# Moving the second column half of a batched FFN from the middle steps of an eight-item pipeline to its start and end

## Chip, cores and metric

The kernel runs on one core of one Trainium2 chip. The metric is the device time of one execution in microseconds (us), as the median of three runs.

## The reference

Eight items of 256 tokens and 256 features pass through one "macaron" block each:

```
x = x + 0.5 * ffn(layernorm(x))                   # first FFN
x = x + attn(layernorm(x))                        # mamba mixer, then a gated MLP (1024 wide)
x = x + 0.5 * ffn(layernorm(x))                   # second FFN, same weights as the first
ffn(x) = sum over 32 experts of combine[t,e] * (silu(x wg_e) * (x wu_e)) wd_e   # top 6 of 32, 96 wide
         + (silu(x sg) * (x su)) sd                                             # shared, 192 wide
```

combine is made from the sigmoid of x @ gate_w: the six largest of the 32 scores, divided by their sum. The mamba mixer has an input projection, a causal convolution of four taps, a recurrence over the tokens with 16 states for each of 512 channels, a gate, and an output projection. All of it is float32.

## The kernel before

**Layout.** Features lie on the partitions, tokens on the free axis, so one item is a tile of 128 x 2 x 256. The FFN is computed densely: 26 chunks of 128 hidden units (24 routed, 2 shared). For each chunk TensorE makes a gate half and an up half, 6 matmuls each (L737 to L739: the weight and the input are each split in a high and a low part, three products, two k blocks), ScalarE takes the tanh (L980) and copies the up half (L970), VectorE applies the gate (L1107, item by_g), GpSimd multiplies by the up half (L1376, by_u) and by the routing weight (L1384, by_comb), and TensorE adds the down projection into the two banks acc (L818; each of the two shows as 2 records, 4 per chunk). All of these work on columns `spans[s.n]` of tiles that are 512 columns wide: 256 columns are one item's call, 512 columns are two calls side by side that share the weights. Below, "narrow" is 256 columns and "wide" is 512.

**Steps.** items_of(t) gives the order of work of step t, for t from -1 to 9. Item i's stages are spread over steps: its first FFN (call f1) in step i, its mamba part in step i+1, its MLP and later its second FFN (call f2 or f2a) in steps i+2 and i+3. So in a middle step four items are in work. Two lists, the heavy one (MLP, then FFN) and the light one (mamba, norms, routing), are merged by fixed weights (merge, WEIGHT, SPACE), and every engine follows the merged order strictly, with a fixed lag for VectorE and GpSimd.

The column slots are filled like this:

| step | columns | first slot | second slot | other work |
|---|---|---|---|---|
| 0 | 256 | f1 of item 0 | - | the FFN weights arrive and are split (ws), the halves go to DRAM (keep_w) |
| 1 | 512 | f1 of item 1 | f1 of item 2 | mamba of item 0 with its own front; no MLP |
| 2 | 256 | f1 of item 3 | - | mamba of item 1 with its own front, first half of item 2's front, MLP of item 0 |
| 3 to 6 | 512 | f1 of items 4 to 7 | f2 of items 0 to 3 | mamba, first half of the next item's front, MLP |
| 7 | 512 | f2a of item 5 | f2 of item 4 | the same; f2a needs the MLP of its own step, a norm and a routing first |
| 8 | 256 | f2a of item 6 | - | mamba of item 7, MLP of item 6, norm and routing |
| 9 | 256 | f2a of item 7 | - | MLP of item 7, norm and routing |

The "front" of an item is what comes before its recurrence: norms lnA or lnO and rms1 or rmsO, projections (L885), convolution, softplus. It has two halves, front(0) and front(1). front(0, "own") stands at the head of a step, before its units, because the item's first FFN ended only with the step before. front(0, "next") stands among units 16 to 31 of the step before. The recurrence is 32 units (ub and unit: L912, L1262, L1069, L1271, L915, L1277, L1397). Items 0 to 7 are read and normed ahead of their first FFN (norm ln1 and ln1b, routing of 8 short pieces on VectorE).

**x1.** The result of the first FFN is added to x. For steps 0 and 1 it lies in x1. The later ones are made in x1_next and moved to x1 by an SBUF to SBUF transfer in the next step (item "shift", L707), which waits until the residual base res has been read (r0, L1153); then x for the next item is loaded to x1_next (again_n, L711). x2kept holds an item between its MLP and its second FFN.

**Queues.** SyncE issues all transfers but the MLP weights, in the order of the merged list: input, weight halves (L672), fronts' spreads (L680 to L689), shift and again_n, stores. GpSimd issues the MLP weights.

Of the kernel before, what the change touches and what calls it, by code (L numbers as in the profile page):

```python
# [67 lines left out]
    "again_n": {"x_again_n": 16},  # L68
    "shift": {"shifted": 16},
# [51 lines left out]
STARTS = {"x2_free": 16}  # L121
# [30 lines left out]
def routing(call):  # L152
    return [("rt1", call)] + [("rq", call, i) for i in range(len(ROUTE))]
# [59 lines left out]

def items_of(t):


    if t < 0:
        return [("load", 0)] + norm("ln1") + routing("f1")
# [3 lines left out]

    first, twin, second, own = t < BATCH - 1, t == 1, 3 <= t < BATCH, t >= BATCH - 1
    late_front, next_front = 1 <= t <= 2, 2 <= t < BATCH
    ready = (["f1"] if first else []) + (["f2"] if twin or second else [])
    hand = [("hx", call) for call in ready] + [("rt2", call) for call in ready]
    following = t == 0 or t + 2 < BATCH
    keep = [("keep",)] if second else []  # L230
    keep += [("load", 0)] if following else []
# [4 lines left out]
    ln1 = norm("ln1") + routing("f1") if following else []  # L236
    if t == 0:
        ln1 = ln1[:2] + [("load", 1)] + ln1[2:] + norm("ln1b") + routing("f2")
    ahead = [(k, c) for c in range(MSLOTS) for k in ("mgn", "mdn")] if 0 <= t + 1 - 2 < BATCH else []
    ff = ffn_items(t)  # L240
    if not mamba:
        if t == 0:
            return hand + keep + merge(ff[:-TAIL], turn + ln1, WEIGHT) + ahead + ff[-TAIL:]
        return mlp_items() + ahead + norm("ln2a") + routing("f1") + [("rt2", "f1"), ("hx", "f1")] + ff
    follow = norm("lnA") + norm("rms1") + merge(front(0, "next"), ln2, SPACE) if next_front else ln2
    light = norm("lnO") + norm("rmsO") + front(0, "own") if late_front else []
    begin = len(light)
# [3 lines left out]
    turns = [("end", "mlp")] if mlp else []  # L251
    turns += [("nm", "lnO")] if late_front else []
    if not mlp:
        out = hand + keep + merge(ff[:-TAIL], light, WEIGHT) + ahead + ff[-TAIL:]
    elif own:
        chain = mlp_items() + ahead + norm("ln2a") + routing("f1") + [("rt2", "f1"), ("hx", "f1")]
        cut = begin + len(unit_items(0) + front(1, "own")) * 2 // 3
        out = hand + keep + merge(chain, light[:cut], WEIGHT) + merge(ff[:-TAIL], light[cut:], WEIGHT) + ff[-TAIL:]
    else:
        heavy = mlp_items() + ahead + ff  # L260
        out = hand + heavy[:6] + keep + merge(heavy[6:-TAIL], light, WEIGHT) + heavy[-TAIL:]
    out = near(after(out, turn, *turns))
    if next_front:

        at = out.index
        assert at(("shift",)) < at(("n1", "lnA")) and at(("ub", UNITS // 2)) < at(("split", 0, "next"))
        assert at(("yz", 1)) < min(at(("xc", 0, "next", 0)), at(("z", 0, "next")))
# [55 lines left out]
def ffn_items(t):  # L323
# [6 lines left out]
    for p in range(FFN_CHUNKS + DLAG):  # L330
        now, before = p < FFN_CHUNKS, 1 <= p <= FFN_CHUNKS
        out += [("cmb", "ff", p // 3)] if p < ROUTED and p % 3 == 0 else []
        out += [("g", "ff", p)] if now else []
        out += [("by_u", "ff", p - 1)] if before else []
        out += [("by_comb", "ff", p - 1)] if 1 <= p <= ROUTED else []
# [10 lines left out]
    if t < BATCH - 1:  # L346
        out += [("end", "f1" if t < 2 else "f1n")]
    if t == 1:
        out += [("end", "f1b")]
    if 3 <= t < BATCH:  # L350
        out += [("end", "f2"), ("store",)]
    return out + ([("end", "f2a"), ("store_own",)] if t >= BATCH - 1 else [])


# [80 lines left out]
def macaron_kernel(nc, d):  # L435
# [8 lines left out]
    spans = [(0, 2 * SEQ if t == 1 or 3 <= t < BATCH else SEQ) for t in times]  # L444
# [3 lines left out]
    with ctx:  # L448
# [29 lines left out]
        x1_next = sb("x1_next", [P, KC, SEQ])  # L478
# [38 lines left out]
        parts = sb("parts", [P, PARTS, 2, SEQ], BF16)  # L517
        rows = nc.dram_tensor("rows", [3, P, PARTS, 2, SEQ], BF16, kind="Internal").ap()
# [105 lines left out]
        def _(sp):  # L624
# [6 lines left out]
            def do(s, it):  # L631
                if it[0] == "load":
# [87 lines left out]
            sp.wait_ge(sem["x2_free"], STARTS["x2_free"] + 16 * BATCH)  # L720
# [3 lines left out]
        def _(pe):  # L724
# [18 lines left out]
            def do(s, it):  # L743
# [77 lines left out]
                elif kind_of(it) == "n1c":  # L821
# [4 lines left out]
                    elif it[1] == "lnA":  # L826
                        pe.wait_ge(sem["shifted"], s.count("shifted", ("shift",), 16))
# [18 lines left out]
                elif kind == "rt1":  # L846
                    if s.n == 0:
                        pe.wait_ge(w_small, 16 * 4)
                    norm = next(n for n in NORMS_OF[it[1]] if ("nm", n) in s.at)
                    pe.wait_ge(sem["normed"], s.count("normed", ("nm", norm), 1))  # L850
# [9 lines left out]
                elif kind == "rt2":  # L860
# [6 lines left out]
                    for tt in range(TT):  # L867
# [615 lines left out]
```

## Time and profile before

| | |
|---|---|
| median of 3 runs | 1793.62 us (1792.89 to 1794.39) |
| the profiled execution | 1797.3 us, span 1795.5 us from first to last instruction |
| PE busy | 1556.8 us, 87% |
| DVE busy | 1288.6 us, 72% |
| POOL busy | 993.8 us, 55% |
| ACT busy | 842.9 us, 47% |
| mean granted TensorE clock | 0.947 |
| bytes moved | 200.25 MB, mean 112 GB/s |

PE is TensorE's matmuls, PEld its weight loads (they overlap PE), DVE VectorE, ACT ScalarE, POOL GpSimd, SPq SyncE's queue of transfers. Busy PE time is modelled and includes stretches at half clock. A step is taken here from the end of the FFN's residual of the step before (L1133) to its own. The next heading's rows are word for word from the profile; L737 is line 737 of the kernel above.

### The profile page before, as it was taken

To read this page: it belongs to the slowest core of one execution; us is meant where nothing else is said; L and a number is where in the kernel's file an instruction comes from. 1 tells how busy PE (TensorE), PEld (TensorE's weight loads), DVE (VectorE), ACT (ScalarE), POOL (GpSimd) and SP (SyncE) were. 2 spreads that over 40 slices of the span, in tenths; PEclk is the share of its full clock that TensorE was granted. 3 is DMA by queue.
4 is the path that set the end of the run, shared out by engine and by line. 5 is a ranking of instruction groups with operands and counts; after the bars stand their busy time and mean duration, and the time that the engine had idled before them with its cause. 6 is when DMAs were issued, how large, how long until landed. Compare 5 with 4: busy or idle time off the path is not lost. (4 is left out here: it accounts for less than half of the span.)

```text
span 1795.5 us, 22504 instructions
## 1 busy us (share of the span) xinstructions
PE 1556.8 (87%) x7088; PEld 1136.3 (63%) x7088; DVE 1288.6 (72%) x2085; ACT 842.9 (47%) x1676; POOL 993.8 (55%) x1048
## 2 busy tenths in 40 slices
PE   6878888777788999899998999899985999868979
PEld 5756555655676666666666666666663666647868
DVE  4536995478968878687959887887857776679421
ACT  4434543545624563356534663456433553445323
POOL 2523676345545766376646666476633766348525
PEclk9989999978989999999999999999996999979989
DMA  6863223332332323242333223232321332224434
GB/s 220 318 206 98 78 82 101 96 100 85 101 105 90 115 84 110 70 138 78 111 102 118 83 90 112 85 129 84 105 79 41 123 100 102 82 86 158 145 104 147
DMA packets 72278, 200.25 MB, mean 112 GB/s; under 512 B 9921, under 2 KB 22433, under 8 KB 71777
## 3 DMA queue, kind: packets, MB, share of 16 engines
q1 hardware_dynamic: 63968, 173.65, 29.1%
q0 software_dynamic: 8192, 25.17, 4.8%
q8 instruction: 57, 0.93, 0.2%
q14 instruction: 61, 0.49, 0.1%
HBM read 173.62 MB, written 23.59 MB: 110 GB/s over the span
## 5 line engine op out<-in xcount | busy, mean ns | idle before, releaser
L737 PE MATMUL gub<-x_hi,wr 128*128 128x512 f32 (+1 forms) x1040 | 425.4, 409 | 50.6 <-DVE hid L1107 44.8
L1397 POOL TENSOR_TENSOR ring<-ring 128x512 f32<-128x512 f32 x192 | 253.6, 1321 | 307.4 <-DVE ring L1277 306.2
L1376 POOL TENSOR_TENSOR hid<-hid,u_sb 128x512 f32<-128x512 f32 (+1 forms) x260 | 289.6, 1114 | 236.1 <-ACT u_sb L970 199.0
L818 PE MATMUL acc<-hid,w_down 128*128 128x512 f32 (+1 forms) x1040 | 408.9, 519 | 1.8 <-POOL hid L1376 1.8
L739 PE MATMUL gub<-x_hi,wr 128*128 128x512 f32 (+1 forms) x1040 | 370.8, 357 | 0.0
L738 PE MATMUL gub<-x_lo,wr 128*128 128x512 f32 (+1 forms) x1040 | 370.2, 356 | 0.0
L1271 DVE TENSOR_TENSOR_SCAN ring<-decays,side 128x512 f32<-128x512 f32 x256 | 310.5, 1213 | 28.9 <-ACT decays L1069 24.6
L970 ACT ACTIVATE u_sb<-gub 128x512 f32<-128x512 f32 (+1 forms) x260 | 132.7, 510 | 347.3 <-PE gub L739 346.8
L980 ACT ACTIVATE hid<-gub 128x256 f32<-128x256 f32 (+1 forms) x324 | 156.8, 484 | 278.2 <-PE gub L739 153.7
L1384 POOL TENSOR_TENSOR hid<-hid,weight 128x512 f32<-128x512 f32 (+1 forms) x240 | 272.9, 1137 | 15.8
L737 PEld LDWEIGHTS gub<-x_hi,wr 128*128 128x128 f32 x1040 | 205.4, 197 | 93.6 <-issue 58.1
L818 PEld LDWEIGHTS acc<-hid,w_down 128*128 128x128 f32 x1040 | 189.2, 197 | 97.2 <-issue 80.8
L1069 ACT ACTIVATE decays<-dts,a_neg 128x255 f32<-128x255 f32 x512 | 228.8, 497 | 3.8 <-DVE ring L1271 3.6
L1262 DVE TENSOR_TENSOR side<-dtx,side 128x512 f32<-128x512 f32 x256 | 176.8, 690 | 69.0 <-PE side L912 68.3
L739 PEld LDWEIGHTS gub<-x_hi,wr 128*128 128x128 f32 x1040 | 204.6, 197 | 27.1
L738 PEld LDWEIGHTS gub<-x_lo,wr 128*128 128x128 f32 x1040 | 205.8, 198 | 24.4 <-issue 5.5
L1107 DVE SCALAR_TENSOR_TENSOR hid<-hid,gub 128x512 f32<-128x512 f32 (+1 forms) x260 | 149.0, 573 | 98.3 <-ACT hid L980 98.3
L1277 DVE TENSOR_TENSOR ring<-ring,side 128x512 f32<-128x512 f32 x256 | 176.0, 687 | 59.5 <-PE side L915 36.2
L885 PE MATMUL side<-rn,w_in 128*128 128x256 f32 x448 | 120.4, 417 | 18.7 <-DVE ring L1271 13.5
L912 PE MATMUL side<-bst,sel_b 96*128 96x256 bf16 x512 | 103.7, 285 | 33.9 <-DVE ring L1271 18.1
L915 PE MATMUL side<-cst,sel_c 96*128 96x256 bf16 x512 | 103.9, 286 | 33.2 <-DVE ring L1271 32.7
L779 PE MATMUL gub<-xn_mlp,wm_gu 128*128 128x256 f32 x512 | 122.4, 387 | 0.0
(120 smaller groups left out, 1823.3 us busy)
## 6 DMA issues: line engine op xcount, KB each, us to landing
wr<-w_halves SPq DMA_DIRECT2D x234, 512.0 KB, 3.3
wm_gu<-in_w_mlp POOLq DMA_DIRECT2D x64, 256.0 KB, 3.1
w_halves<-wr SPq DMA_DIRECT2D x26, 512.0 KB, 4.9
wm_down<-in_w_mlp POOLq DMA_DIRECT2D x64, 128.0 KB, 2.6
w_raw<-in_w_gu SPq DMA_DIRECT2D x26, 256.0 KB, 4.3
rows<-parts SPq DMA_DIRECT2D x16, 384.0 KB, 2.3
cst<-rows SPq DMA_DIRECT2D x48, 128.0 KB, 2.6
xin<-in_x SPq DMA_DIRECT2D x8, 256.0 KB, 2.9
```

Source lines behind the costliest of these rows:

```text
L737: mm(out, w[:, 0, half, k, :], x_hi[:, k, a:b], start=(k == 0), stop=False)
L738: mm(out, w[:, 0, half, k, :], x_lo[:, k, a:b], start=False, stop=False)
L739: last = mm(out, w[:, 1, half, k, :], x_hi[:, k, a:b], start=False, stop=(k == KC - 1))
L818: last = mm(acc[k][:, a:b], w, h[:, a:b], start=(c == 0), stop=(c == (MLP_CHUNKS if mlp else FFN_CHUNKS) - 1))
L980: A(hid[c % HSLOTS][:, a:b], s.gub_of(it)[:, a:b], ACT.Tanh, scale=0.5).then_inc(sem["tanh_done"], 1)
L1069: A(decay[u % 2][:, h, 1:SEQ], dts[:, j, 1:SEQ], ACT.Exp, scale=a_neg[:, j, n:n + 1]).then_inc(sem["decay"], 1)
L1262: v.tensor_tensor(b, twice(dtx[:, j, :]), b, ALU.mult).then_inc(sem["driven"], 1)
L1271: v.tensor_tensor_scan(w.rearrange("p h s -> p (h s)"), decay[u % 2][:, :, :].rearrange("p h s -> p (h s)"), s.side_of(("ub", u))[:, :], 0 ...
L1277: v.tensor_tensor(w, w, pair(s.side_of(it)), ALU.mult).then_inc(sem["read_out"], 1)
L1376: nc.gpsimd.tensor_tensor(h, h, u_sb[c % USLOTS][:, a:b], ALU.mult).then_inc(sem["hidden"], 1)
L1384: nc.gpsimd.tensor_tensor(h, h, weight[c // 3 % CSLOTS][:, a:b], ALU.mult).then_inc(sem["weighted"], 1)
L1397: add(ysum, ysum, ring[:, u % 3], ALU.add).then_inc(sem["y_sum"], 1)
```

## The change

The columns are dealt out anew. Items 0 to 5 have their first FFN in pairs, in steps 0, 1 and 2, at 512 columns. Steps 3 to 8 run at 384 columns: one slot of a whole item and one of half an item's tokens (128). Step 9 stays at 256.

| step | columns before | columns after | calls after |
|---|---|---|---|
| 0 | 256 | 512 | f1 of items 0, 1 |
| 1 | 512 | 512 | f1 of items 2, 3 |
| 2 | 256 | 512 | f1 of items 4, 5 |
| 3, 4 | 512 | 384 | half of f1 of item 6, f2 of items 0, 1 |
| 5, 6 | 512 | 384 | half of f1 of item 7, f2 of items 2, 3 |
| 7 | 512 | 384 | half of f2 of item 5 (its own MLP first), f2 of item 4 |
| 8 | 256 | 384 | half of f2 of item 5, f2 of item 6 (its own MLP first) |
| 9 | 256 | 256 | f2 of item 7 |

With items 0 and 1 both ready after step 0, front(0, "next") starts in step 1, and only step 1 still has front(0, "own"). The norms and routings that must be ready move too: items 0 and 1 before step 0 (their routing inside step 0), 2 and 3 in step 0, 4 and 5 in step 1, 6 in step 2, 7 in step 4. x1 of all items but item 0 goes to a DRAM tensor x1_kept (store_a, store_b at a step's end) and comes back by a transfer "fetch" at the place of shift. x for the residual is loaded at the head of steps (again_a, again_b). The memset of x2kept at the start is gone.

```
+FIRST = {0: (0, 1), 1: (2, 3), 2: (4, 5), 3: (6,), 4: (6,), 5: (7,), 6: (7,)}
+NORMED_IN = {-1: (0, 1), 0: (2, 3), 1: (4, 5), 2: (6,), 4: (7,)}
+OWN_SLOT = {BATCH - 1: "f1", BATCH: "f2", BATCH + 1: "f1"}
+def half_of(t):
+    return (t - 3) % 2 if 3 <= t <= BATCH else None
+def span_of(t):
+    return (0, 2 * SEQ) if t < 3 else (P, 2 * SEQ) if t <= BATCH else (0, SEQ)
+def place(t, slot):
+    if slot == "f2":
+        return slice(SEQ, 2 * SEQ), slice(0, SEQ)
+    half = half_of(t)
+    return (slice(0, SEQ), slice(0, SEQ)) if half is None else (slice(P, SEQ), slice(half * P, half * P + P))
...
-    late_front, next_front = 1 <= t <= 2, 2 <= t < BATCH
+    next_front = 1 <= t < BATCH
...
-    turn += [("again",)] if t < 2 else [("shift",)] if t < BATCH else []
-    turn += [("again_n",)] if 1 <= t < BATCH - 1 else []
+    turn += [("fetch",)] if next_front else []
...
+    if t == 0:
+        early = [it for call in ("f1", "f2") for it in routing(call, ("early",)) + [("rt2", call)]]
+        at = ff.index(("cmb", "ff", 0))
+        return near(fetches + hand + merge(ff[:at], early, WEIGHT) +
+                    merge(ff[at:-TAIL], ln1, WEIGHT) + ahead + ff[-TAIL:])
...
+        late = splits and p < 3
+        if late and p == 2:
+            out += [("cmb", "ff", 0), ("by_comb", "ff", 0), ("by_comb", "ff", 1)]
...
-    spans = [(0, 2 * SEQ if t == 1 or 3 <= t < BATCH else SEQ) for t in times]
+    spans = [span_of(t) for t in times]
...
-                if it[0] == "shift":
+                if it[0] == "fetch":
                     sp.wait_ge(sem["r_base"], s.count("r_base", ("r0",), 1))
-                    sp.dma_start(x1[:], x1_next[:]).then_inc(sem["shifted"], 16)
+                    stored = "b_stored" if s.t() in (1, 3, 5) else "a_stored"
+                    sp.wait_ge(sem[stored], s.prior(stored))
+                    sp.dma_start(x1[:], x1_kept[s.t()]).then_inc(sem["fetched"], 16)
+                if it[0] == "again_a":
+                    if (least := s.prior("a_stored")) is not None:
+                        sp.wait_ge(sem["a_stored"], least)
+                    sp.dma_start(x1_stage[:], d["x"][FIRST[s.t()][0]]).then_inc(sem["x_again_a"], 16)
+                if it[0] == "store_a":
+                    sp.wait_ge(sem["residual"], s.count("residual", ("end", "f1n"), KC))
+                    sp.dma_start(x1_kept[FIRST[s.t()][0]], x1_stage[:]).then_inc(sem["a_stored"], 16)
...
-            v.memset(x2kept[:], 0.0).then_inc(sem["x2_free"], STARTS["x2_free"])
...
-                        v.scalar_tensor_tensor(dst[:, k, :], acc[k][:, a:a + SEQ], scale, src[:, k, :],
+                        v.scalar_tensor_tensor(dst[:, k, tokens], acc[k][:, cols], scale, src[:, k, tokens],
```

## Rows read from the trace of the kernel before

**Rows 1.** Windows by step: length, busy PE PEld DVE ACT POOL, PEclk, DMA share, GB/s.

```profile
0.00:116.00 116.00, 84.89 (x478) 75.68 (x478) 50.00 (x136) 47.82 (x106) 42.96 (x54) 0.93 0.75 259
116.00:314.90 198.90, 171.62 (x674) 111.72 (x675) 144.65 (x210) 93.81 (x177) 113.00 (x98) 0.95 0.30 98
314.90:528.60 213.70, 160.56 (x826) 132.29 (x825) 162.91 (x270) 104.72 (x218) 95.49 (x118) 0.87 0.31 98
528.60:727.60 199.00, 185.16 (x784) 126.80 (x784) 159.66 (x251) 101.28 (x191) 121.90 (x118) 0.99 0.30 97
...
1125.70:1324.60 198.90, 182.29 (x764) 123.87 (x763) 155.62 (x228) 97.79 (x185) 122.10 (x118) 0.99 0.31 99
1324.60:1537.70 213.10, 187.43 (x764) 127.76 (x764) 152.07 (x227) 97.66 (x185) 121.37 (x118) 0.94 0.28 91
1537.70:1694.00 156.30, 123.90 (x714) 103.13 (x712) 120.73 (x196) 67.35 (x158) 90.37 (x118) 0.89 0.36 117
...
sum 1793.20, PE 1556.78 PEld 1136.32 DVE 1288.56 ACT 842.89 POOL 993.75; mean PE 155.68 PEld 113.63 DVE 128.86 ACT 84.29 POOL 99.38
```

**Rows 2.** Windows of stretches inside steps; same columns.

```profile
361.50:436.80 75.30, 55.42 (x294) 44.34 (x293) 66.20 (x104) 34.73 (x79) 37.66 (x39) 0.82 0.31 100
436.80:507.60 70.80, 53.79 (x297) 44.65 (x298) 63.70 (x101) 41.67 (x88) 36.31 (x38) 0.88 0.29 94
507.60:528.60 21.00, 16.16 (x82) 13.75 (x81) 10.98 (x20) 5.68 (x10) 6.62 (x8) 0.92 0.31 104
528.60:567.20 38.60, 29.70 (x139) 23.65 (x139) 29.90 (x53) 15.00 (x32) 12.76 (x25) 0.96 0.18 52
567.20:618.70 51.50, 51.05 (x224) 34.37 (x221) 49.12 (x78) 28.40 (x55) 42.99 (x43) 1.00 0.43 141
618.70:700.90 82.20, 78.61 (x330) 51.68 (x330) 67.55 (x102) 49.75 (x93) 54.96 (x43) 1.00 0.30 97
700.90:727.60 26.70, 25.80 (x96) 17.09 (x95) 13.09 (x22) 8.13 (x12) 11.19 (x10) 1.00 0.24 79
1125.70:1158.40 32.70, 26.88 (x132) 21.26 (x131) 27.12 (x49) 14.43 (x33) 12.50 (x24) 0.97 0.25 72
...
1386.80:1537.70 150.90, 149.14 (x592) 99.68 (x592) 102.67 (x133) 72.53 (x135) 97.57 (x76) 0.98 0.31 103
...
1600.00:1694.00 94.00, 83.52 (x543) 72.90 (x542) 73.33 (x107) 42.57 (x108) 66.66 (x76) 0.96 0.47 155
```

**Rows 3.** Timeline of PE, narrow call: start, length, what.

```profile
1760.10 1.02 PE L818 MATMUL acc<-hid,w_down 128*128 128x256 f32 x4
...
1762.39 1.02 PE L818 MATMUL acc<-hid,w_down 128*128 128x256 f32 x4
```

**Rows 4.** Timeline of PE, wide call.

```profile
640.51 0.39 PE L737 MATMUL gub<-x_hi,wr 128*128 128x512 f32 x1
640.74 0.39 PE L738 MATMUL gub<-x_lo,wr 128*128 128x512 f32 x1
...
643.04 1.88 PE L818 MATMUL acc<-hid,w_down 128*128 128x512 f32 x4
644.76 1.89 PE L885 MATMUL side<-rn,w_in 128*128 128x256 f32 x8
```

**Rows 5.** Groups by line and shape, DVE: busy us, mean ns, idle before.

```profile
L1107 DVE SCALAR_TENSOR_TENSOR hid<-hid,gub 128x512 f32<-128x512 f32 x156 | 105.9, 679 | 32.9 <-ACT hid L980 32.9
...
L1107 DVE SCALAR_TENSOR_TENSOR hid<-hid,gub 128x256 f32<-128x256 f32 x104 | 43.1, 415 | 65.3 <-ACT hid L980 65.3
```

**Rows 6.** Timeline of the start, three instructions.

```profile
4.24 2.04 PE L835 MATMUL side<-xin,mean_w 128*128 128x256 f32 x4 [4.24 <-DMA xin<-in_x]
...
12.21 0.69 DVE L1176 TENSOR_TENSOR xc_f<-xc_f,rstd 128x512 f32<-128x512 f32 x1 [5.13 <-ACT rstd L998]
...
22.32 0.78 PE L737 MATMUL gub<-x_hi,wr 128*128 128x256 f32 x1
```

**Rows 7.** Waits in 22 to 116 us: total us, times, longest.

```profile
ACT wr L949 <- DMA w_raw<-in_w_gu: 19.5, 7, 5.1
```

More of the change, by code:

```diff
@@ L67 @@
     "again": {"x_again": 16},
-    "again_n": {"x_again_n": 16},
-    "shift": {"shifted": 16},
+    "again_a": {"x_again_a": 16},
+    "again_b": {"x_again_b": 16},
+    "store_a": {"a_stored": 16},
+    "store_b": {"b_stored": 16},
+    "fetch": {"fetched": 16},
     "hx": {"x_hi": 1, "x_split": 1},
@@ L119 @@
 }
[L121 removed]
+STARTS = {}
 def kind_of(item):
@@ L214, in items_of @@
 def items_of(t):
     if t < 0:
-        return [("load", 0)] + norm("ln1") + routing("f1")
+        ln1 = norm("ln1")
+        return [("load", 0)] + ln1[:2] + [("load", 1)] + ln1[2:] + norm("ln1b")
     mamba, mlp = 0 <= t - 1 < BATCH, 0 <= t - 2 < BATCH
-    first, twin, second, own = t < BATCH - 1, t == 1, 3 <= t < BATCH, t >= BATCH - 1
-    late_front, next_front = 1 <= t <= 2, 2 <= t < BATCH
-    ready = (["f1"] if first else []) + (["f2"] if twin or second else [])
-    hand = [("hx", call) for call in ready] + [("rt2", call) for call in ready]
@@ L229, in items_of @@
-    following = t == 0 or t + 2 < BATCH
-    keep = [("keep",)] if second else []
-    keep += [("load", 0)] if following else []
+    own = OWN_SLOT.get(t)
+    next_front = 1 <= t < BATCH
+    ready = [slot for slot in ("f1", "f2") if slot != own and t <= BATCH]
+    hand = [("hx", call) for call in ready]
+    hand += [("rt2", call) for call in ready] if t else []
+    keep = [("keep",)] if 3 <= t <= BATCH else []
+    fetches = ([("again",), ("again_b",)] if t == 0 else [("again_a",), ("again_b",)] if t < 3 else
+               [("again_a",)] if t in (3, 5) else [])
@@ L239, in items_of @@
+    ln1 = [("load", 0)] + ln1 if ln1 else []
+    if t in NORMED_IN and len(NORMED_IN[t]) > 1:
+        ln1 = ln1[:3] + [("load", 1)] + ln1[3:] + norm("ln1b") + routing("f2")
     ahead = [(k, c) for c in range(MSLOTS) for k in ("mgn", "mdn")] if 0 <= t + 1 - 2 < BATCH else []
     ff = ffn_items(t)
[L241 to L244, printed above, removed]
+    if t == 0:
[3 more added lines that the diff above has]
+                    merge(ff[at:-TAIL], ln1, WEIGHT) + ahead + ff[-TAIL:])
@@ L245, in items_of @@
+    chain = []
+    if own:
+        chain = (norm("ln2a") + routing("f1") if own == "f1" else norm("ln2") + routing("f2")) + [
+            ("rt2", own), ("hx", own)]
+        chain = mlp_items() + ahead + chain
+        if not mamba:
+            return chain + ff
     follow = norm("lnA") + norm("rms1") + merge(front(0, "next"), ln2, SPACE) if next_front else ln2
-    light = norm("lnO") + norm("rmsO") + front(0, "own") if late_front else []
-    begin = len(light)
+    light = norm("lnO") + norm("rmsO") + front(0, "own") if t == 1 else []
@@ L265, in items_of @@
         at = out.index
-        assert at(("shift",)) < at(("n1", "lnA")) and at(("ub", UNITS // 2)) < at(("split", 0, "next"))
+        assert at(("fetch",)) < at(("n1", "lnA")) and at(("ub", UNITS // 2)) < at(("split", 0, "next"))
         assert at(("yz", 1)) < min(at(("xc", 0, "next", 0)), at(("z", 0, "next")))
@@ L826, in do @@
                     elif it[1] == "lnA":
-                        pe.wait_ge(sem["shifted"], s.count("shifted", ("shift",), 16))
+                        pe.wait_ge(sem["fetched"], s.count("fetched", ("fetch",), 16))
                     elif it[1] == "lnO":
@@ L846, in do @@
                 elif kind == "rt1":
[L847 removed]
+                    if s.n == 1:
                         pe.wait_ge(w_small, 16 * 4)
[L849 to L850 removed]
+                    pe.wait_ge(sem["normed"], s.count("normed", it, 0))
                     for over, least in s.last_use("side", it):
```

90 lines of the change are left out of this document (50 added, 40 removed).

## The prediction

> **What bounds the kernel now.** I read the windows by step first. Over the ten steps PE is busy 1557 of 1793 us and DVE 1289 [rows 1], so the means name TensorE. The steps differ. Step 3 has PE busy 185 of 199 us, and step 6, with fewer DVE instructions (228 against 251), takes the same 198.9 us: those wide middle steps follow PE. Step 2 computes half as many FFN columns and still takes 213.7 us, with PE at 161 and DVE at 163. Steps 0 and 8 are narrow too and have PE idle for 31 and 32 us. So columns are crowded where PE has no slack and missing where it has.
>
> Then the stretches inside a step [rows 2]. Step 3 (start at 528.6) has four: MLP until the first FFN matmul, 38.6 us with DVE at 29.9 and PE at 29.7, a chain of short dependent pieces, bound by neither; 51.5 us up to scan 16, where PE is 99% and DVE 95% busy; 82.2 us up to scan 31 with PE at 96% and DVE at 82%; a tail of 26.7 us with PE at 97%. The same three last stretches of step 2, narrow, take 75.3 (all of units 0 to 15), 70.8 and 21.0 us, and in the first two DVE is at 88 and 90%, PE at 74 and 76%. So at 256 columns the units are bound by VectorE, at 512 by TensorE, and 384 lies near the crossing. That is the question of this change.
>
> **What a column costs.** Narrow chunks follow each other by 2.29 us on a dense PE (start of one chunk's down matmuls to the next's, 12 gate and up matmuls between) [rows 3]. Wide: gate and up matmuls start 0.23 us apart, and four down records take 644.76 - 643.04 = 1.72 us [rows 4], so a chunk is 12 x 0.23 + 1.72 = 4.48 us. 26 chunks: 59.5 us narrow, 116.5 us wide. That is linear in columns with nearly no fixed part, so 384 columns are estimated halfway, 88 us, and no weight load sets a floor. The change keeps ten FFN passes and 4096 columns in all. PE's work is the same to a microsecond: all that can be won or lost is idle time. The term on DVE, by_g, is 679 ns wide and 415 narrow [rows 5], so 547 at 384: 26 x 0.132 = 3.4 us less per step.
>
> **Step 0, 256 to 512 columns.** Before, the FFN waits for weights (19.5 us of ScalarE waiting for w_raw [rows 7], DMA share 0.75 [rows 1]): 90 us for 59.5 us of PE work. Wide, PE needs 116.5, plus some 2 us of routing-weight matmuls and 7.5 us for two norms and four routings, 126 us, longer than the 90 us in which the weights came; they are hidden. The start is later: the first norm's chain runs from 4.24 to 12.9 us [rows 6], the second follows with its ScalarE part behind the first, about 8 us, then two splits (1.1 us each) and the first weight split: first gate matmul near 24 instead of 22.3. Routing of both calls is moved behind the first matmuls. End: 24.5 + 126/0.96 + 3 = 158 against 116. **+42** (37 if PE never waits, 50 if weights still cost 8).
>
> **Step 1, still 512.** It gains front(0, "next") and a second norm with routing. What that costs DVE is read from steps 1 and 2: step 2 has those same two things (its second norm is ln2) and the MLP's 16 gatings, and is narrow by 26 x 0.264 = 6.9 us, which the MLP's 16 x 0.42 = 6.7 offsets. So step 1 gets step 2's DVE load, 162.9 us instead of 144.7, while PE goes from 172 to about 184. With step 2's ratio of span to DVE time (213.7/162.9) it takes 214, with step 1's own (198.9/144.7) 224; I take 217, nearer the lower as the kinds of work are step 2's. **+18** (8 if it is PE at 184/0.89 = 207, 30 if the added chain is bare).
>
> **Step 2, 256 to 512.** The own front leaves its head. What is left is step 3's list but for f1 in the second slot. 199. **-14.7** (-12 to -16).
>
> **Steps 3 to 6, 512 to 384.** PE loses 28.5 us per step, 1.1 per chunk; DVE 3.4. By stretches: MLP 38.6, unchanged. To scan 16, ten chunks: PE 51 - 11 = 40, DVE 49.1 - 1.3 = 48; DVE binds, 50 us (-1.5). To scan 31, twelve chunks: PE 78.6 - 13 = 65.5, DVE 67.6 - 1.6 = 66. Bounds: 82.2 (nothing won) and 66/0.95 = 69.5, 0.95 being DVE's share in the stretch before; step 2's DVE share of 0.90 gives 73. I take 72 (-10). Tail: midway of 26.7 and 21.0, 24 (-3). Sum 184.5. Three of the four steps no longer hold a first norm: step 6, which has none, has an MLP stretch of 32.7 instead of 38.6 [rows 2], lost again later to PE before. Now PE has room, so I count 5 of those 6: 179.5. Four steps: 184.5 + 3 x 179.5 = 723 against 796. **-73** (-92 if stretches meet their DVE floor at once, -39 by the clock, below).
>
> **Step 7, 512 to 384.** From the first FFN matmul on, 150.9 us with PE at 149.1 and DVE only at 102.7 [rows 2]. PE goes to 120.6, DVE to 99. At 95% of PE: 127. **-24** (-28 to -15). **Step 8, 256 to 384.** From 1600 on, 94 us with PE at 83.5; PE goes to 112, over 0.97: 115.5. **+22** (18 to 28.5, the whole of the added work). **Step 9**: 0.
>
> **x1 by DRAM.** Fetch stands where shift stood, behind the same wait for r0, and moves the same 256 KB. What waits for it is lnA, among units 16 to 31, some 60 us later. The stores at a step's end queue ahead of again_a and again_b (each waits for a store to land, a few us) and those ahead of weight loads whose chunks are 6 ahead, at least 13 us. Cover: 38 us of MLP in steps 3 to 7; in steps 1 and 2 the slots already filled. Cost 0; if the cover failed, 2 to 4 us in each of two steps. again_n's load, which stood before a weight load right after shift, is gone from there.
>
> **Sum.** 42 + 18 - 15 - 73 - 24 + 22 = -30. The profiled span of 1795.5 becomes 1766; its own time was 1797.3, the median 1793.6. Taking 30 from the median: **1764 us**.
>
> **Rivals.** (1) Clock. In step 2's narrow unit stretches the granted clock is 0.82 and 0.88, in step 3's wide ones 1.00 [rows 2]: a PE left with gaps falls between its two levels of 2.4 and 1.2 GHz, and the same matmul takes twice as long. If 384 columns leave gaps like step 2's, the stretches become 40/0.82 = 49 to 52 us, 65.5/0.88 = 74.4 to 77, tail 25: 192.6 and 188 without the norm, four steps 757. The sum is -30 + 34 = +4: **1798**, slower. It decides if the four steps lose less than 9 us each on average. Against it: PE would be 80% busy there, more than step 2's 75%, and DVE's 66 us leave room for a slowed PE up to 0.99 of it. The Trainium skill, "TensorE: Matmul & The Clock Gate", section "HAM oscillation", says that a kernel whose matmul bursts are separated by short idle gaps keeps falling back to half rate; by that rule alone the sum would be this rival's. The trace agrees at 256 columns and shows none of it at 512; no row is at 384. (2) DVE and PE, near balance under a fixed order that was weighted for 512 columns, hinder each other: the long stretch stays at 78, steps 3 to 6 give 45 to 50: **1785** or so. For it: step 2 never reaches 0.95 of DVE. Against: step 3 has both at 95 and 99% for 51 us. (3) PE bound all along: units shrink to their DVE floor, the full MLP saving stays, steps 3 to 6 give 92: **1746**. (4) Zero sum: what steps 3 to 7 give, steps 0, 1 and 8 take, as PE's work is the same: **1793**. Against it is the 31 us of idle PE in step 0 and the front that leaves step 2's head.
>
> **Chances.** My sum, within 11 us: 0.47. Rival 3 side (1735 to 1753): 0.14. Rival 2 side (1775 to 1790): 0.23. Rival 4: 0.06. Rival 1: 0.10. Range 1745 to 1789; the likeliest alone 1753 to 1775. A difference of 0.2% (3.6 us) is what a measurement of this kernel can tell. Faster 0.84, same 0.06, slower 0.10.
>
> **What would show it.** Right: step 0 near 158 us with PE dense; step 1 near 217; step 2 at 199; steps 3, 5, 6 at 180 and step 4 at 185, DVE at 90% or more up to scan 31; step 7 at 189, step 8 at 178; fetch landing long before lnA. Wrong: PEclk under 0.92 in steps 3 to 6; the stretch to scan 31 near 80 us; step 1 over 225; SPq's weight loads late after again_a.

## The result: slower by 2.1% where a gain of 1.7% was forecast

| | before | after |
|---|---|---|
| median | 1794.01 us | 1831.60 us (1826.90 to 1834.43) |
| ratio | | 1.0206, 95% interval 1.0183 to 1.0230 |
| profiled span | 1795.5 us | 1829.6 us |
| mean granted clock | 0.947 | 0.944 |

The forecast was 1764 with a range of 1745 to 1789. The change made the kernel 38 us slower. The sign was wrong, and rival 1, the only one with that sign, gave 1798.

The windows by step of the changed kernel, cut as [rows 1] are, at the end of the FFN's residual (length; then busy PE, PEld, DVE, ACT, POOL; PEclk, DMA share, GB/s):

```profile
0.00:159.80 159.80, 139.84 (x496) 93.97 (x496) 77.19 (x164) 67.09 (x112) 71.02 (x54) 0.99 0.59 198
159.80:391.10 231.30, 190.06 (x739) 127.15 (x740) 168.51 (x257) 115.39 (x210) 115.10 (x98) 0.93 0.26 86
391.10:605.70 214.60, 194.34 (x777) 131.96 (x776) 162.62 (x250) 101.32 (x191) 120.93 (x118) 0.94 0.30 98
605.70:790.50 184.80, 159.12 (x768) 123.87 (x767) 148.13 (x228) 90.56 (x185) 107.56 (x118) 0.97 0.33 107
790.50:992.00 201.50, 168.69 (x778) 130.17 (x777) 154.63 (x252) 94.93 (x191) 107.61 (x118) 0.92 0.30 99
992.00:1175.80 183.80, 159.88 (x768) 124.86 (x767) 147.99 (x229) 90.74 (x185) 107.61 (x118) 0.96 0.33 107
1175.80:1364.40 188.60, 159.34 (x761) 123.77 (x760) 150.62 (x228) 90.00 (x185) 107.42 (x118) 0.96 0.32 104
1364.40:1553.50 189.10, 161.70 (x767) 126.84 (x766) 146.94 (x228) 90.98 (x185) 107.49 (x118) 0.92 0.32 103
1553.50:1727.30 173.80, 148.33 (x717) 115.59 (x716) 127.45 (x203) 74.26 (x158) 103.97 (x118) 0.92 0.32 104
...
sum 1827.20, PE 1569.33 PEld 1177.99 DVE 1309.64 ACT 844.90 POOL 992.06; mean PE 156.93 PEld 117.80 DVE 130.96 ACT 84.49 POOL 99.21
```

Set beside the forecast step by step, most of the ledger holds. Step 0 is 159.8 (forecast 158) with PE dense, step 7 is 189.1 (189), step 8 is 173.8 (178), steps 3 and 5 are 184.8 and 183.8 (179.5). The error sits in four steps: step 1 at 231.3 (217), step 2 at 214.6 (199), step 4 at 201.5 (184.5), step 6 at 188.6 (179.5). Step 2 is the telling one. It was to be a copy of step 3 before, the same number of columns and the same work, 199.0 us [rows 1], and it takes 15.6 us more with a clock of 0.94 against 0.99. Steps 3 and 6 do the same work as each other and differ by 3.8 us. In sum the steps are 64 us over the forecast span of 1766: step 0 by 2, step 1 by 14, step 2 by 16, steps 3 to 6 by 36, step 8 under it by 4.

### The profile page after: what moved, and what is told of

The parts are those of the page before. It is cut to its first block and busy times, and to the rows that moved or that the text cites. A ratio compares the mean times of both kernels' runs of the same rounds, so it can differ in the third digit from the quotient of the medians.

```text
span 1829.6 us, 22541 instructions
## 1 busy us (share of the span) xinstructions
PE 1569.3 (86%) x7088; PEld 1178.0 (64%) x7088; DVE 1309.6 (72%) x2100; ACT 844.9 (46%) x1676; POOL 992.1 (54%) x1048
## 5 line engine op out<-in xcount | busy, mean ns | idle before, releaser
L789 PE MATMUL gub<-x_hi,wr 128*128 128x384 f32 (+2 forms) x1040 | 435.0, 418 | 36.5 <-DVE hid L1158 33.8
L1435 POOL TENSOR_TENSOR hid<-hid,u_sb 128x384 f32<-128x384 f32 (+2 forms) x260 | 288.7, 1110 | 253.6 <-ACT u_sb L1022 246.7
L870 PE MATMUL acc<-hid,w_down 128*128 128x384 f32 (+2 forms) x1040 | 404.5, 514 | 0.4 <-POOL hid L1435 0.4
L791 PE MATMUL gub<-x_hi,wr 128*128 128x384 f32 (+2 forms) x1040 | 372.4, 358 | 0.0
L790 PE MATMUL gub<-x_lo,wr 128*128 128x384 f32 (+2 forms) x1040 | 372.1, 358 | 0.0
L1022 ACT ACTIVATE u_sb<-gub 128x384 f32<-128x384 f32 (+2 forms) x260 | 132.3, 509 | 363.2 <-PE gub L791 362.7
L1032 ACT ACTIVATE hid<-gub 128x384 f32<-128x384 f32 (+2 forms) x324 | 156.9, 484 | 301.8 <-PE gub L791 165.6
L1443 POOL TENSOR_TENSOR hid<-hid,weight 128x384 f32<-128x384 f32 (+2 forms) x240 | 271.6, 1132 | 20.8 <-ACT weight L1012 5.6
L789 PEld LDWEIGHTS gub<-x_hi,wr 128*128 128x128 f32 x1040 | 203.3, 196 | 74.4 <-issue 50.1
L1158 DVE SCALAR_TENSOR_TENSOR hid<-hid,gub 128x384 f32<-128x384 f32 (+2 forms) x260 | 149.1, 574 | 90.0 <-ACT hid L1032 89.9
L791 PEld LDWEIGHTS gub<-x_hi,wr 128*128 128x128 f32 x1040 | 202.6, 195 | 14.2
L937 PE MATMUL side<-rn,w_in 128*128 128x256 f32 x448 | 118.4, 412 | 15.0 <-DVE ring L1330 13.4
```

What stands on the lines that cost most here:

```text
L789: mm(out, w[:, 0, half, k, :], x_hi[:, k, a:b], start=(k == 0), stop=False)
L790: mm(out, w[:, 0, half, k, :], x_lo[:, k, a:b], start=False, stop=False)
L791: last = mm(out, w[:, 1, half, k, :], x_hi[:, k, a:b], start=False, stop=(k == KC - 1))
L870: last = mm(acc[k][:, a:b], w, h[:, a:b], start=(c == 0), stop=(c == (MLP_CHUNKS if mlp else FFN_CHUNKS) - 1))
L1032: A(hid[c % HSLOTS][:, a:b], s.gub_of(it)[:, a:b], ACT.Tanh, scale=0.5).then_inc(sem["tanh_done"], 1)
L1435: nc.gpsimd.tensor_tensor(h, h, u_sb[c % USLOTS][:, a:b], ALU.mult).then_inc(sem["hidden"], 1)
```

## What the trace shows first: a load that stands right in front of its reader

The instructions on the tile xin, the item read for the first norm, in the changed kernel (the matmul row; then the DMA whose landing ended idle time before these instructions, the idle us and how often):

```profile
L887 PE MATMUL side<-xin,mean_w x32: 377/558/796, 4.2 to 852.4; 128*128 128x256 f32 x32
...
  DMA xin<-in_x: 28.6, 8
```

and in the kernel before:

```profile
L835 PE MATMUL side<-xin,mean_w x32: 377/379/765, 4.2 to 984.5; 128*128 128x256 f32 x32
...
  DMA xin<-in_x: 4.2, 1
```

Before, the one wait for this transfer is that of the first instructions. After, the idle time counts PE and its weight loads; of PE alone it is 4.2 us at the start and then 3.9, 2.4 and 5.1 us in steps 1, 2 and 4, the only steps behind step 0 that have such norms. Step 4 after, timeline of SyncE and then of PE (start, length, what):

```profile
843.35 1.63 SPq L711 DMA_DIRECT2D wr<-w_halves  x3
845.02 0.43 SPq L678 DMA_DIRECT2D xin<-in_x  x1
```

```profile
851.00 2.07 PE L887 MATMUL side<-xin,mean_w 128*128 128x256 f32 x4 [5.06 <-DMA xin<-in_x]
852.86 0.64 PE L964 MATMUL side<-bst,sel_b 96*128 96x256 bf16 x2
853.29 2.77 PE L870 MATMUL acc<-hid,w_down 128*128 128x384 f32 x4
```

The same step before, SyncE and PE:

```profile
727.99 0.44 SPq L639 DMA_DIRECT2D xin<-in_x  x1
```

```profile
785.51 1.02 PE L835 MATMUL side<-xin,mean_w 128*128 128x256 f32 x4
```

Before, 57 us lie between the issue and the reader. After, the load is issued behind three weight loads and PE stands still for 5.1 us. Everything behind the norm in PE's order stands with it: the unit's and the FFN's matmuls. The four matmuls then take 2.07 us instead of 1.02, with a granted clock of 0.50 from 851 to 853 us, the lower of the two levels. It is in a part of the diff that the core shown above leaves out and that the prediction does not speak of: `keep += [("load", 0)]` at the head of the step is gone, and `ln1 = [("load", 0)] + ln1` puts the load into the light list.

The second thing shows in the order of work itself. The last items of each FFN list, which are kept out of the merge, are `TAIL = 6` items in both kernels. The new store items (store_a, store_b) are among them:

```
step 4 before, last six:  down 23, down 24, down 25, end f1n, end f2, store
step 4 after,  last six:           down 24, down 25, end f1n, store_a, end f2, store
```

So in steps 1, 2, 4 and 6 one more down item goes into the merge (in step 1 the item by_u 25 too), all positions of the heavy list shift by a fraction, and near ties fall the other way. Between step 3 before (373 items) and step 2 after (374), 173 lines of the lists are removed or added. (The 273 and 35 of an expectation below count the diff's own head lines too; without them they are 173 and 21.) Of the 32 units, 11 stand right in front of a by_g before and 6 after, and 14 instead of 8 stand right behind an up half:

```
step 3 before:  rq, rq, unit 14, by_g 7, u 7, rq, wl, g 8
step 4 after:   rq, rq, by_g 7, u 7, unit 14, wl, g 8, rq
```

## The experiments

### Is it the load or the order? (four kernels)

Edit of the first, on the changed kernel, with `keep` also placed in step 1's list:

```
-    ln1 = [("load", 0)] + ln1 if ln1 else []
+    if t == 0 and ln1:
+        ln1 = [("load", 0)] + ln1
+    elif ln1:
+        keep += [("load", 0)]
```

> The changed kernel, but in steps 1, 2 and 4 the load of x for the first norm stands at the head of the step again, not right in front of the norm that reads it. In the changed kernel TensorE stood 3.9, 2.4 and 5.1 us before that norm's matmuls (steps 1, 2, 4), with half clock around each. Theory L (the late load is what made steps 1, 2 and 4 long, by 14 to 17 us over my forecast each): 1832 falls by 30 to 45 us, to about 1795; step 2 at 200, step 4 at 186. Theory O (the order of the merged list slipped, because the four closing items of these steps leave two real items instead of three in the unmerged tail): only the stalls themselves go, 4 to 7 us per step, 1832 falls by 10 to 20; step 2 stays over 207, step 6, which has no load, stays 5 us over steps 3 and 5 in both.

Edit of the second, on the changed kernel:

```
+    TAIL = 3 + len(ff) - next(i for i, it in enumerate(ff) if it[0] == "end") if 1 <= t <= 6 else 6
```

> The changed kernel, but the unmerged tail of steps 1 to 6 always holds three down items and the closing items, so that steps 2, 4 and 6 get nearly the order of the middle steps before (step 2 differs from step 3 before in 35 lines instead of 273). Theory O: steps 2, 4 and 6 fall to about 203, 190 and 184, step 1 by 5 to 10, in sum 30 us, to about 1802. Theory L: only step 6 changes, by at most 5 us; total within 6 us of 1832.

The third has both edits.

> Both edits of the two runs before. If load and order add up and are the whole of what I missed in steps 1 to 6: step 1 at 217, step 2 at 199, step 4 at 185 to 188, steps 3, 5 and 6 at 184, total about 1785, faster than the kernel before. If the step lengths of 384 columns are set by the clock or by DVE and PE hindering each other: steps 3 to 6 do not come under 188 in the mean and the total stays over 1800.

The fourth takes the late load alone to the kernel before.

```
-    keep += [("load", 0)] if following else []
+    keep += [("load", 0)] if t == 0 else []
+    ln1 = [("load", 0)] + ln1 if ln1 and t else ln1
```

> The kernel before, with one thing of the change alone: in steps 1 to 5 the load of x stands right in front of the first norm instead of at the step's head (5 loads). Theory L: 5 steps by 8 to 15 us each, total slower by 40 to 70. Theory O: the stall alone, 3 to 6 us per step, slower by 15 to 30. If the late load were harmless in wide steps: no change.

| kernel | median us | ratio to before (95%) | steps 1, 2, 3, 4, 5, 6 in us |
|---|---|---|---|
| the change | 1831.6 | 1.0206 (1.0183, 1.0230) | 231.3, 214.6, 184.8, 201.5, 183.8, 188.6 |
| load at the head | 1816.1 | 1.0119 (1.0096, 1.0141) | 225.9, 208.6, 185.0, 194.8, 183.7, 188.6 |
| tail of three | 1803.3 | 1.0050 (1.0033, 1.0066) | 225.1, 205.7, 182.2, 193.1, 185.0, 184.6 |
| both | 1799.3 | 1.0031 (1.0020, 1.0041) | 227.3, 200.3, 184.9, 188.1, 183.7, 184.3 |
| before, load late | 1816.8 | 1.0123 (1.0102, 1.0143) | 204.8, 213.7, 205.8, 204.8, 204.5, 198.9 |

The medians are of the runs of each kernel, the steps of one profiled execution. How far a step scatters can be seen where kernels share its list: step 2 with both repairs is 199.0 to 202.4 us in six kernels of this document, step 1 227.3 to 231.3 in four.

Both causes are real. Taken alone, the load's place costs 5.4, 6.0 and 6.7 us in steps 1, 2 and 4 of the change (15.5 in the median), and in the kernel before 5.0 to 6.8 us in each of the four steps 1, 3, 4 and 5 (22.5 in the median). There, step 2 does not move (213.7 both times), though its load was late too. The idle time itself, 2.4 to 5.1 us, is somewhat under what the step loses. That is theory O's size for the load, so theory L as the whole cause falls. The tail gives 28.3 us, 4.0 of it in step 6, which has no load, 8.9 in step 2, 8.4 in step 4 and 6.2 in step 1. Together they give 32.3, less than 43.8, the sum of the two: each also hides part of the other. In step 1 the two do not add at all (5.4 and 6.2 alone, 4.0 together), and the scatter of that step is 4. With both repaired step 2 is at 200.3 against my 199:

```profile
161.10:388.40 227.30, 186.24 (x734) 123.98 (x735) 170.04 (x257) 115.36 (x210) 115.30 (x97) 0.95 0.26 85
388.40:588.70 200.30, 185.80 (x786) 126.98 (x785) 158.23 (x250) 101.30 (x191) 122.55 (x120) 0.99 0.33 106
588.70:773.60 184.90, 162.28 (x764) 126.15 (x763) 148.21 (x229) 90.73 (x185) 107.78 (x118) 0.94 0.33 108
773.60:961.70 188.10, 163.29 (x781) 125.80 (x780) 155.50 (x252) 94.20 (x191) 107.42 (x118) 0.96 0.32 105
```

(windows of the kernel with both edits, steps 1 to 4). Of the 14.3 us that step 2 loses in the change (214.6 against 200.3), 8.5 are PE busy time (194.34 against 185.80) at a granted clock of 0.94 in place of 0.99, the rest is idle time.

The total, 1799.3, is still 35 us over the forecast. 1785 was expected of this kernel if the two causes were all, and over 1800, with steps 3 to 6 at 188 or more in the mean, for a floor by clock or hindrance. Steps 2 to 6 meet the first expectation within 1.3 us; the total lies near the second because step 1 takes 227.3 and not 217. Step 4 by the forecast's own stretches (MLP, to scan 16, to scan 31, tail; forecast 38.6, 50, 72 and 24):

```profile
773.60:812.90 39.30, 31.15 (x138) 24.46 (x137) 29.95 (x54) 14.99 (x32) 13.09 (x25) 0.91 0.22 67
812.90:862.10 49.20, 44.49 (x225) 33.79 (x222) 46.75 (x77) 25.51 (x55) 38.24 (x44) 0.97 0.42 142
862.10:937.40 75.30, 66.19 (x335) 51.04 (x335) 65.49 (x102) 46.42 (x94) 46.82 (x42) 1.00 0.32 106
937.40:961.70 24.30, 21.45 (x89) 16.50 (x88) 13.30 (x22) 7.28 (x12) 9.26 (x10) 0.93 0.26 87
```

### Is it PE, a floor, or the order at 384 columns? (four kernels)

All four stand on the kernel with both repairs. In the first the merge weights of the FFN in steps 3 to 8 are cut as the columns were:

```
+    W = {**WEIGHT, "g": 1.0, "u": 1.0, **{("down", "ff", c): 1.3 for c in range(FFN_CHUNKS)}} if t >= 3 else WEIGHT
-        out = hand + heavy[:6] + keep + fetches + merge(heavy[6:-TAIL], light, WEIGHT) + heavy[-TAIL:]
+        out = hand + heavy[:6] + keep + fetches + merge(heavy[6:-TAIL], light, W) + heavy[-TAIL:]
```

(the same in steps 7 and 8.) No instruction is added or left out; only the order of the engines' work changes. Lower weights crowd the FFN's items together and move units ahead of them: in step 3's list seven units stand in front of the first FFN gate with both repairs, eight with weights down, five with the weights up of the second kernel.

> The kernel of both repairs, and the merge weights of the FFN items in steps 3 to 8 cut from 1.3, 1.3 and 1.7 (gate, up, down) to 1.0, 1.0, 1.3, as their columns were cut. Theory B (my rival 2: the fixed order was weighted for 512 columns and hinders the engines at 384): steps 3 to 6 fall from 185 to 180 or less, 1799 to under 1785, faster than the kernel before. Theory F (a floor of VectorE and dependent chains, whatever the order): steps 3 to 6 stay within 2 us of 185, or grow as more units stand in the MLP stretch; total 1795 to 1805.

The second has 1.7 and 2.2 in place of 1.0 and 1.3.

> The same, with the weights raised to 1.7, 1.7 and 2.2, so that fewer units stand in the MLP stretch. Theory B: slower, steps 3 to 6 at 188 or more. Theory F: within 2 us of 185 too, or shorter if the MLP stretch was overfull; total 1790 to 1805.

The third:

```
-    return (0, 2 * SEQ) if t < 3 else (P, 2 * SEQ) if t <= BATCH else (0, SEQ)
+    return (0, 2 * SEQ) if t < 3 else (SEQ, 2 * SEQ) if t < 7 else (P, 2 * SEQ) if t <= BATCH else (0, SEQ)
```

> The kernel of both repairs, with the FFN of steps 3 to 6 at 256 columns in place of 384: the halves of items 6 and 7 are left out of it, their residual adds what the bank held. TensorE loses another 28.5 us per step, VectorE 3.4 us. If TensorE still sets the 384 column steps: 20 to 28 us less per step, total near 1700. If the floor of VectorE and chains is reached at 384 (rival 2, or the clock): 2 to 8 us less per step, 177 to 183, total 1770 to 1790. The clock rival says besides that the granted clock falls under 0.92 in these steps.

The fourth:

```
-        ln1 = ln1[:cut] + [("load", 1)] + ln1[cut:] + norm("ln1b") + routing("f2")
+        ln1 = ln1[:cut] + [("load", 1)] + ln1[cut:] + (norm("ln1b") + routing("f2") if t == 0 else [])
```

> The kernel of both repairs without the second norm and routing of step 1 (ln1b and its routing, of item 5, whose first FFN then works on item 3's values). I put step 1 at 217 and it is 227. If VectorE's load sets the step: 8 us less in step 1, 219, total 1791. If it is the added front half with its chain and PE's waits: 0 to 3 us less.

| kernel | median us | ratio to before (95%) | steps 1, 3, 4, 5, 6 in us |
|---|---|---|---|
| both repairs (from above) | 1799.3 | 1.0031 (1.0020, 1.0041) | 227.3, 184.9, 188.1, 183.7, 184.3 |
| weights down | 1765.5 | 0.9842 (0.9811, 0.9872) | 227.4, 173.7, 187.4, 173.9, 173.8 |
| weights up | 1789.5 | 0.9976 (0.9962, 0.9991) | 231.3, 179.2, 197.4, 178.5, 178.0 |
| 256 columns in steps 3 to 6 | 1755.0 | 0.9780 (0.9755, 0.9805) | 227.8, 172.6, 179.4, 175.2, 172.1 |
| one norm in step 1 | 1787.2 | 0.9957 (0.9942, 0.9973) | 221.7, 183.1, 184.0, 184.4, 184.4 |

Steps 3 to 6 with weights down, and for comparison step 5 of the kernel with both repairs:

```profile
589.00:762.70 173.70, 154.96 (x763) 121.36 (x762) 146.37 (x229) 90.64 (x185) 109.30 (x118) 0.98 0.35 115
762.70:950.10 187.40, 163.91 (x781) 126.47 (x780) 156.49 (x252) 94.83 (x191) 107.83 (x118) 0.95 0.32 105
950.10:1124.00 173.90, 157.06 (x765) 123.08 (x764) 146.90 (x229) 90.63 (x185) 108.99 (x118) 0.97 0.35 115
1124.00:1297.80 173.80, 157.06 (x764) 123.07 (x763) 146.73 (x228) 90.63 (x185) 108.97 (x118) 0.97 0.34 112
```

```profile
961.70:1145.40 183.70, 158.50 (x765) 123.35 (x764) 147.85 (x229) 90.53 (x185) 107.47 (x118) 0.97 0.33 109
```

Two of these steps with 256 columns:

```profile
590.10:762.70 172.60, 134.39 (x764) 112.54 (x763) 142.15 (x228) 83.15 (x185) 93.57 (x118) 0.93 0.35 116
762.70:942.10 179.40, 144.88 (x781) 119.88 (x780) 149.45 (x252) 87.80 (x191) 93.85 (x118) 0.90 0.34 110
```

With the same work in another order, steps 3, 5 and 6 fall by 10 to 11 us, to 174. That beats my 179.5, and the whole kernel, at 1765.5, lands on the forecast and 1.6% under the kernel before. The clock is not what changed in step 5: it is 0.97 in both, PE is busy 158.5 and 157.1 us, and the step is 9.8 us shorter, so what went is idle time. The 256 column kernel keeps the order weights of the repaired one and leaves out an estimated 28.5 us more of PE's work per step. Its steps fall by 8.5 to 12.3 us, more than the 2 to 8 expected of a floor (1755.0 in all against 1770 to 1790) and far less than the 20 to 28 of a step set by TensorE. So with that order PE's work was not the main thing that set these steps. The granted clock is 0.93, 0.90, 0.92 and 0.93 there, around the 0.92 under which the clock rival had put it. That steps 3, 5 and 6 come to nearly the same time with weights down at 384 columns (173.7 against 172.6) fits a floor of VectorE and its chains near 173, but does not show it: PE is then busy 89% of step 3 and VectorE 84%, and 256 columns with weights down were not run. What is shown is that this order of the list cost 10 us a step at the same work.

The stretches of step 3 show where the order mattered. First the change, then weights down, from the first FFN matmul to scan 16 and from there to scan 31:

```profile
640.50:683.90 43.40, 37.99 (x197) 28.98 (x195) 41.84 (x57) 21.07 (x47) 34.17 (x39) 1.00 0.44 149
683.90:767.90 84.00, 71.84 (x347) 56.01 (x346) 68.08 (x103) 48.16 (x96) 51.60 (x47) 0.96 0.31 101
```

```profile
624.10:664.30 40.20, 36.05 (x179) 28.79 (x178) 35.93 (x51) 17.96 (x42) 32.31 (x37) 0.92 0.45 152
664.30:738.90 74.60, 69.35 (x353) 54.38 (x352) 65.53 (x103) 47.88 (x97) 52.01 (x47) 1.00 0.34 112
```

The last stretch of the change, 84.0 us, is longer than the 82.2 of the wide step 3 before [rows 2], with a quarter fewer FFN columns: PE busy 86%, DVE 81%, neither at its limit. With weights down it is 74.6, PE 93% and DVE 88%. I had put it at 72. The cuts do not part the same work: without a first norm more units stand in the MLP stretch, so the stretch to scan 16 is shorter than my 50 in both (43.4 and 40.2). The change's step 3 as a whole misses the forecast by 5.3 us, not by the 12 of this stretch, and in step 4, where the units stand as I had counted them, the four stretches with both repairs are within 3.3 us of the forecast's.

My own theory B did not come out as written. It said that weights should shrink with the columns, and weights up should be slower, 188 or more. Weights up gave 178.5 in steps 3, 5 and 6, faster than the repaired kernel as well, and 197.4 in step 4, slower. So there is no simple law "weights in proportion to columns" here. The order of the two repairs was a poor one for 384 columns and both others happened to be better where no first norm is in the step. Theory F is refuted for steps 3, 5 and 6. Step 4 did not move with weights down (188.1 to 187.4), but the same theory said within 2 us with weights up too, and there it grew by 9.3.

The one-norm kernel takes 5.6 us off step 1, between the two expectations (8, and 0 to 3), and VectorE's busy time there falls from 170.0 to 163.6 us. With a scatter of 4 us in this step the runs do not decide between the two, and why step 1 exceeds my 217 by 10 us stays open. Step 4, whose list that edit leaves alone, also came out at 184.0 against 188.1, so part of this kernel's 12 us is not due to its edit.

### Controls: is the order before special, and how much is owed to the columns? (four kernels)

The first puts the same weights down into the kernel before. The second shortens the tail of the kernel before in steps 3 to 6:

```
+    TAIL = 5 if 3 <= t <= 6 else 6
```

The third is the change as it stood, with late load and short tail, and weights down. The fourth is the best kernel with weights down in step 1 too.

> The kernel before, with the FFN's merge weights cut to 1.0, 1.0, 1.3 in steps 3 to 8, nothing else. It asks whether the 28 us between the last two schedules are the columns' or the order's. If the order before was well fitted to 512 columns and the gain is owed to 384: steps 3 to 6 at 199 or more, total 1790 to 1815. If the new weights are simply better: faster by 10 us or more.

> The kernel before, with the unmerged tail of steps 3 to 6 one item shorter, so that two down items stand in it instead of three, the slip that the change brought to steps 1, 2, 4 and 6. Theory O: each of the four steps grows by 4 to 9 us, total slower by 16 to 36. If the slip only matters beside the late load or at 384 columns: within 5 us of before.

> The change as it stood, late load and short tail kept, with the weights cut in steps 3 to 8. If weights alone repair it: steps 3, 5 and 6 at 174 to 178, total about 1800. The late load should still cost 5 to 6 us in each of steps 1, 2 and 4, and step 1 stay at 231, so I expect 1795 to 1805.

> The best kernel so far (1765.5) with the cut weights in step 1 too. Step 1 is the one step left far off my forecast (227 against 217). If its order is as poor as that of steps 3 to 6 was: 217 to 222, total 1757 to 1760. If DVE's load of 170 us with the front's chain sets it: within 3 us of 227, total 1763 to 1768.

| kernel | median us | ratio to before (95%) | steps 1, 3, 4, 5, 6 in us |
|---|---|---|---|
| before | 1793.1 | 1 | 198.9, 199.0, 199.8, 198.3, 198.9 |
| before, weights down | 1801.5 | 1.0048 (1.0031, 1.0065) | 202.4, 200.6, 205.4, 203.7, 192.7 |
| before, tail of two | 1817.5 | 1.0122 (1.0088, 1.0157) | 200.4, 203.6, 204.6, 204.7, 203.4 |
| the change, weights down | 1785.4 | 0.9949 (0.9930, 0.9968) | 230.4, 174.5, 194.4, 174.5, 173.8 |
| best, weights down in step 1 | 1766.5 | 0.9846 (0.9820, 0.9872) | 234.6, 171.9, 188.2, 172.9, 173.0 |

The table's first row has the steps of the profile that the prediction was made from. Steps 3 to 6 of the kernel before with the short tail:

```profile
526.20:729.80 203.60, 187.03 (x781) 128.38 (x780) 159.88 (x251) 101.30 (x191) 120.90 (x118) 0.97 0.29 95
729.80:934.40 204.60, 187.83 (x782) 128.62 (x781) 159.65 (x251) 101.30 (x191) 121.58 (x118) 0.97 0.30 97
934.40:1139.10 204.70, 188.05 (x782) 128.75 (x781) 159.73 (x252) 101.29 (x191) 121.58 (x118) 0.97 0.30 98
1139.10:1342.50 203.40, 183.95 (x764) 125.17 (x763) 159.00 (x228) 97.30 (x185) 121.94 (x118) 0.98 0.30 97
```

DVE and PE have the same instructions as in [rows 1] (DVE busy 159.9 against 159.7 us in step 3, PE 187.0 against 185.2), and each step is 4.5 to 6.4 us longer. So a slip of one list item is worth 5 us per step in the kernel before as well: theory O stands by itself, without the load and without 384 columns.

Weights down make the kernel before 0.5% slower in sum. So the gain of the best kernel is not one that this change of weights would have given the old column plan. But the first expectation, every step at 199 or more, fails in step 6:

```profile
1141.20:1333.90 192.70, 182.91 (x764) 125.20 (x763) 155.59 (x229) 97.43 (x185) 122.30 (x118) 0.98 0.31 102
```

That is 6.2 us less than before with the same work, at 512 columns, while steps 3, 4 and 5 grow by 1.6 to 5.6. Step 6 is the one of the four without a first norm. At 384 columns too, the steps without one gain (10 to 11 us) and the one with it does not. So a part of what weights down give is owed to what else stands in the step and not to 384 columns; the new plan has three such steps and the old one had one.

The change with weights down, 1785.4, is 10 us under the least that I expected (1795). Steps 3, 5 and 6 came as expected. Step 6 is at 173.8 with its short tail, as it is without (173.8): the slip that cost it 4 us under the old weights costs nothing under the new ones. Weights alone give 46.2 of the 68 us and the two repairs behind them 19.9, where the repairs first gave 32.3 and the weights behind them 33.8: what each is worth depends on which is made first. Even with its late load and short tail the change beats the kernel before by 0.5% in this order.

In step 1 weights down did not help: 234.6 against 227.4, outside both expectations (217 to 222, or within 3 of 227), though the total, 1766.5, lies in the second one's range.

## Why the prediction was wrong, by its steps

- **What a column costs: right.** Gate and up matmuls at 384 columns start about 0.17 us apart (707.71 to 707.88 in the kernel with both repairs), halfway between 0.12 (1761.08 to 1761.20 in the kernel before) and 0.23; by_g takes 546 ns for the 547 forecast. PE's work did not change in sum: 7088 matmuls in both, busy 1556.8 us before and 1558.4 with both repairs (1569.3 in the change, at a slightly lower clock).
- **Step 0 (+42): right.** It is 159.8 with a clock of 0.99, PE busy 140. The weights came in its shadow: ScalarE waits 2.1 us for w_raw in place of 19.5.
- **Step 1 (217): too low by 14.** Each repair alone takes some six off (231.3 to 225.9 and to 225.1), both together four (227.3). Some 10 over the forecast remain after both. The term "step 2's DVE load, 162.9" was too small: it is 170.0. How much of the 10 that explains is not shown.
- **Step 2 (199): this is the step of the prediction that failed.** "What is left is step 3's list" is not so. Two items had moved: the load of x from the step's head to its reader, and one down item out of the tail, pushed there by the new store items. I priced neither, although both can be worked out from the diff. The same failure stands in step 4 (17 us over 184.5, of which the repairs take 13.4) and, by the tail alone, in step 6 (4 of 9 us). With both undone step 2 measures 200.3.
- **Steps 3 to 6 (-73): the second failure.** After the change the four steps take 758.7 us (forecast 723, before 796), with both repairs 741, with weights down 708.8. So 18 us of the miss are the slips and 18 remain, mostly in steps 3, 5 and 6 at 184 for 179.5. In their stretches the term "to scan 31, 72" was mis-sized (84.0 in step 3 of the change) and "to scan 16, 50" erred the other way (43.4), in part because units stand elsewhere. Rival 2 (engines that hinder each other under a fixed order) is the mechanism, and its 45 to 50 us for the four steps came near the 55 that they gave with both repairs; its total was added up too low, as these steps make it 1787 to 1792 and not 1785. Weights down then took the same steps 14 us under the forecast.
- **The first norm at 5 us per step: not a constant.** With weights down, step 4 has one and takes 187.4, steps 3, 5 and 6 have none and take 173.8: 13.6 us. At 256 columns the difference is 4.2 to 7.3, in the repaired kernel some 4. Under the same columns it goes from 4 to 14 us with the order alone.
- **Steps 7 and 8: right** (189.1 for 189; 173.8 for 178, four under).
- **x1 by DRAM at cost 0: right for the transfers, wrong for the list.** No compute engine waits for them; they take 2.0 to 5.6 us to land, and the norm that reads them comes 30 us or more behind the landing. This was read from the trace and not tried by an experiment. But the store items that this path needs are what pushed a down item out of the tail, and that slip is worth 28 us alone.
- **Rival 1 (clock): a part of the time, not its cause.** The granted clock in steps 3 to 6 was 0.92 to 0.97 after, not 0.82 to 0.88. It moved with the order at the same matmuls: 0.98 in step 3 with weights down, 0.94 with both repairs. Of the 50 us by which the four steps are longer in the change than with weights down, 14 are PE busy time (647.0 against 633.0 us) and 36 idle time, so slower matmuls are directly at most 14 of them. The rule of the Trainium skill that I set against the change ("TensorE: Matmul & The Clock Gate", section "HAM oscillation") agrees with the stall of step 4, where the clock falls to 0.50; by the rule alone, as I priced it, the total would be 1798, and it is 1831.6.

In the ledger: from 1764 to 1831.6 are 68 us. The two slips of the list account for 32.3 (1831.6 to 1799.3), the order at 384 columns for 33.8 (1799.3 to 1765.5), taken in this sequence. That the last kernel comes within 1.5 us of 1764 is luck and no confirmation of the sum: its steps are off by +10 in step 1, +3 in steps 0 and 4, +1 in step 2, -17 in steps 3, 5 and 6 together and -5 in step 8.

**What stays open:** why step 1 takes 227; why a given order is good or poor for a step. The runs show that it is, by 4 to 11 us a step, and I have no rule that would have said which. That weights down work in steps 3, 5 and 6 is a find and not a derivation. Whether 174 us is the floor of these steps is open too.

## What to carry to other kernels

When an order is written by a list and merged by weights, read what a new item does to the list and not only what it costs itself: a store of 0.3 us, put among the closing items, made three steps 4 to 9 us longer, and a fourth by 6 at most. Check for every load how far it stands in front of its first reader in the issuing queue's order, above all when the diff moves the line that makes it. Where a change brings the engines of a step into balance, forecast the time under the old order apart from the floor, and try some orders before judging the change: here the same column plan is 2.1% slower or 1.6% faster than the kernel before. And an order that helps one kind of step can cost another: judge it step by step.

## What the runs showed of the hardware that was not expected

A load issued right behind weight loads and other transfers lands later: in the kernel before with the load late, the five late loads of xin take 4.2 to 5.9 us from issue to landing, where those of the kernel before that follow only a store take 2.7 (medians of all eight: 4.5 and 2.9). And a stall of PE costs more than its length: the four late loads of steps 1, 3, 4 and 5 there idle PE for 2.4 to 4.9 us and lengthen the steps by 5.0 to 6.8. In the step 4 of the change shown above, 5.1 us of waiting are followed by matmuls at the lower clock level, 2.07 us for four that take 1.02 otherwise, and 10 us around it have a mean granted clock of 0.73:

```profile
845.00:855.00 10.00, 4.94 (x15) 3.31 (x14) 5.03 (x7) 1.59 (x5) 5.43 (x6) 0.73 0.47 179
```
